# Selector products on 96 rows, and low products last behind a wait of their own

## The chip, the cores and the metric

The kernel runs on one core of one Trainium2 chip. The metric is the device time of one execution in microseconds (us). The core's engines are TensorE (PE: matrix products, with its weight loads listed apart as PEld), VectorE (DVE), ScalarE (ACT), GpSimd (POOL) and SyncE (SP, which here only issues DMAs). Each engine works off its own list of instructions in order. They meet only at semaphores: an instruction may wait until a counter has reached a value.

## The reference

Two blocks run one after the other on 64 images of 1024 channels and 14 x 14 points, all in float32. The first is three convolutions with batch norm over the whole batch. The second, in which the change lies, works on each image by itself:

```python
def _L1_conv_ref(x, w1, gn1_scale, gn1_bias, w_off, b_off, w2, gn2_scale, gn2_bias, w3, gn3_scale, gn3_bias, stride):
    out = relu(group_norm(conv(x, w1), gn1_scale, gn1_bias))      # 1024 -> 256 channels
    om = conv(out, w_off, pad=1) + b_off                          # 27 channels, 3x3
    off_x, off_y, mask = om[:, :9], om[:, 9:18], sigmoid(om[:, 18:])
    py, px = grid_y + off_y, grid_x + off_x                       # a point for each tap
    sampled = bilinear_sample(out, py, px) * mask                 # 9 taps
    out = einsum('bckhw,ock->bohw', sampled, w2)                  # deformable 3x3, 256 -> 256
    out = relu(group_norm(out, gn2_scale, gn2_bias))
    out = group_norm(conv(out, w3), gn3_scale, gn3_bias)          # 256 -> 1024 channels
    return relu(out + x)
```

## The kernel before

**Stages.** Three phases do the first block (to about 900 us of the span). `deformable_phase` does the second. It goes through 32 pairs of images; a pair has 2 x 196 = 392 columns.

**Split products.** Each float32 operand is stored as two parts in a matmul type: `hi`, a rounded copy that ScalarE makes, and `lo`, what is left, which VectorE makes as value minus `hi`. So `lo` is always later than `hi`. A product of two operands is three matmuls into one sum: w_hi x_hi, w_hi x_lo, w_lo x_hi. `product3` (lines 69 to 74) issues them in that order; in every view below L72, L73 and L74 are these three. A matmul loads its own stationary operand.

**The steps of a pair on TensorE:**
- `conv1(p, k)`, k = 0 to 7: 1x1 convolution from 1024 to 256 channels, two output tiles of `work`, 6 matmuls for each k. It waits for `x1_lo_made`.
- `offsets`: the 27 channel convolution, into `work`.
- `spread_offsets(p, c)`, c = 0 to 2 (line 1999): one matmul each with 0/1 matrices `select`, which hands each offset channel to the partitions of its taps and rows. Its input `om_parts` has 64 rows: 32 with the high part of the offsets, 32 with the low part. ScalarE then makes from the results the weights of the bilinear sampling ("hats"), and these go through DRAM back into SBUF. There are 3 x 32 = 96 of these matmuls.
- `transposes(p, i)`: four float32 matmuls each, into `work`.
- `sample_tile(p, t)`, t = 0 to 19: bilinear sampling as a product of the activations `aT` with the sampling matrix `s` over 98 rows, 6 matmuls, into one of two banks of `sample`. `s` comes in 9 units a pair: GpSimd multiplies two hats, ScalarE makes `s_hi`, VectorE `s_lo` (L1793). The first tile of each unit (channel half c == 0, 10 tiles a pair) waits for `s_lo_made`. Every tile also waits with `at_least(pe, v_lo_made, ...)` for the bank of `sample` to be read.
- `deform_part(p, g, part)`: the deformable product over two taps (one in the last group), into `deform`. ScalarE makes `v_hi` from `sample` (L1447), VectorE `v_lo` (L1801). Ten of the twenty parts a pair wait for `v_lo_made`.
- `conv3(p, k)`, k = 0 to 7: 256 to 1024 channels, 6 matmuls each. The first of each k waits for `y_written` (its bank of `work` read), the first of all for `b_lo_made` too.
- `group_a`, `group_b`, `group_y`: small matmuls for the group norms (L1123), into `sums_ps`.

**Order.** The order on each engine is written out by hand in its `step` function. One step interleaves parts of four neighbouring pairs, so that while VectorE and ScalarE prepare one thing TensorE has another. `keep_warm` adds matmuls whose results are not used, at the beginning and the end.

In the built program each matmul carries the size of the part of TensorE's array that it uses, as rows x columns. It is 128x128 for all matmuls of the kernel (those with 98 rows in `sample_tile` and those with 96 columns in `offsets` among them), except the 96 of `spread_offsets`, which carry 64x128. 2,283 matmuls have a wait.

Of the kernel before, what the change touches and what calls it, by code (L numbers as in the profile page):

```python
# [14 lines left out]
F32R = mybir.dt.float32r  # L15
# [32 lines left out]
OFFCH = 27  # L48
ONE = 29
# [6 lines left out]
def at_least(eng, sem, value):  # L56

    if not isinstance(value, int) or value > 0:
        eng.wait_ge(sem, value)
# [17 lines left out]
def keep_warm(nc, out, values, count):  # L77

    for _ in range(count):
        nc.tensor.matmul(out, values[:, 0:P], values[:, 0:PAIR], start=True, stop=True)  # L80

# [1077 lines left out]
def deformable_phase(nc, x, y3, before_layer, w1, w2, w3_source, woff_source, consts, hats_at, out, y_home, in_home, y_stored, x1,  # L1159
# [4 lines left out]
    with ExitStack() as ctx:  # L1164
# [36 lines left out]

        a_hi = x1_hi[:].rearrange("p r i s -> p (r i s)")[:, 0:KM * PAIR].rearrange("p (k i s) -> p k i s", k=KM, i=2)
        a_lo = x1_lo[:].rearrange("p r i s -> p (r i s)")[:, 0:KM * PAIR].rearrange("p (k i s) -> p k i s", k=KM, i=2)
        om_parts = x1_hi[0:64, RING - 1].rearrange("p i s -> p (i s)")
# [53 lines left out]
        select, place = consts["select"][0:64, :], consts["select"][64:96, 0:PIX]  # L1258
# [703 lines left out]
        def _(pe):  # L1962
            @of_pair
            def conv1(p, k):
                if k == 0:
                    at_least(pe, aT_lo_made, 2 * p.n - 1)
                    at_least(pe, y_written, KX * (p.n - 2))
                pe.wait_ge(x1_lo_made, KX * p.n + k + 1)
                for t in range(KM):
                    last = product3(nc, work[:, t, 0:PAIR], w1_hi[:, k, t, :], w1_lo[:, k, t, :],  # L1970
                                    x1_hi[:, k % RING].rearrange("p i s -> p (i s)"),
                                    x1_lo[:, k % RING].rearrange("p i s -> p (i s)"),
                                    start=(k == 0), stop=(k == KX - 1))
                last.then_inc(conv1_used, 1)
# [39 lines left out]
            @of_pair  # L2014
            def sample_tile(p, t):
                g, i, c = t // 4, t // 2 % 2, t % 2
                u, n = min(t // 2, UNITS - 1), cols(g)
                at = i * PIX if u == UNITS - 1 else 0
                unit = UNITS * p.n + u
                if t in (0, 2):  # L2020
                    pe.wait_ge(aT_lo_made, 2 * p.n + i + 1)
                if c == 0:
                    pe.wait_ge(s_lo_made, unit + 1)
                at_least(pe, v_lo_made, TILES * p.n + t - 1)
                for h in range(2):
                    last = product3(nc, sample[:, t % 2, 0:n], aT_hi[:, i, h, c * P:(c + 1) * P],
                                    aT_lo[:, i, h, c * P:(c + 1) * P],
                                    s_hi[:, unit % 2, h, at:at + n], s_lo[:, unit % 2, h, at:at + n],
                                    start=(h == 0), stop=(h == 1))
                last.then_inc(sampled, 1)  # L2030

            @of_pair
            def deform_part(p, g, part):
                k, t = divmod(part, 2)
                group = GROUPS * p.n + g
                if t == 0:
                    pe.wait_ge(v_lo_made, TILES * p.n + 4 * g + 3 + k)
                if part == 0 and g == 0:
                    at_least(pe, b_raw, p.n)
                for tap in range(taps_of(g)):  # L2040
                    last = product3(nc, deform[:, t, 0:PAIR], w2_hi[:, k, 2 * g + tap, t, :],
                                    w2_lo[:, k, 2 * g + tap, t, :],
                                    v_hi[:, group % 2, k, tap].rearrange("p i s -> p (i s)"),
                                    v_lo[:, group % 2, k, tap].rearrange("p i s -> p (i s)"),
                                    start=(g == 0 and k == 0 and tap == 0),
                                    stop=(g == GROUPS - 1 and k == KM - 1 and tap == taps_of(g) - 1))
                if t == 1:
                    last.then_inc(deformed, 1)

            @of_pair  # L2050
            def conv3(p, k):
                bank = 2 - k % 2
                if k == 0:
                    if p.n == 0:
                        pe.wait_ge(w3.lo_made, 1)
                    pe.wait_ge(b_lo_made, p.n + 1)
                    pe.wait_ge(aT_lo_made, 2 * min(p.n + 2, PAIRS))
                if k == 1:
                    pe.wait_ge(a_raw, min(p.n + 3, PAIRS))
                at_least(pe, y_written, KX * p.n + k - 1)  # L2060
                for c in range(KM):
                    last = product3(nc, work[:, bank, 0:PAIR], w3_hi[:, c, k, :], w3_lo[:, c, k, :],
                                    b_hi[:, c, :], b_lo[:, c, :], start=(c == 0), stop=(c == KM - 1))
                last.then_inc(conv3_done, 1)
# [110 lines left out]
def build(nc, x, w, vectors, select, ident, ones, b_off, out):  # L2175
# [5 lines left out]
    with ExitStack() as ctx:  # L2181
# [3 lines left out]
        select_s = sb("select_s", [96, 3 * TAPS * SIDE], F32R)  # L2185
# [21 lines left out]
        with ExitStack() as inner:  # L2207
# [22 lines left out]
            stage = in_home[0:96, 0:3 * TAPS * SIDE]  # L2230
# [66 lines left out]
```

## Time and profile before

| what | value |
|---|---|
| three runs | 2995.97, 2997.18, 2997.70 us, median 2997.18 us |
| the profiled execution's own time | 2997.73 us |
| its span, first to last instruction | 2995.6 us |
| PE busy | 2936.5 us (98%), 16,518 matmuls |
| DVE busy | 2374.3 us (79%) |
| ACT busy | 1798.1 us (60%) |
| POOL busy | 717.0 us (24%) |
| mean granted clock of TensorE | 0.993 of full |

The profiled execution lies 0.5 us above the median and 2.1 us above its own span. A matmul of 392 columns is listed with 0.34 us, but the next one starts 0.18 us after it: matmuls overlap, so the distance from start to start, not the busy time, is what one costs. Idle time is counted from the end of one matmul to the start of the next, so a wait listed with 0.57 us moved the next start by more than that.

### The profile page before, as it was taken

The page shows a single profiled execution, that of the slowest core. Times are in us where ns is not written, and L with a number is a line of the kernel's source. Part 1 is how long each engine was busy: PE and PEld are TensorE (multiplying, and loading weights), DVE is VectorE, ACT ScalarE, POOL GpSimd, SP SyncE. Part 2 cuts the span into 40 slices and gives each one's busy share as a digit, 9 for nine tenths or more (in the row PEclk, how much of TensorE's full clock was granted, in tenths as well). Part 3 has the DMA queues.
Part 4 walks back from the last instruction along what each step waited for, and adds up shares of the span by engine and source line. Part 5 has one row for each costly group of instructions (what it writes and reads, how often), then busy time and mean ns, then how long its engine had stood idle before and what let it go on. Part 6 is the DMA issues. An engine that isn't in the chain of part 4 may idle for free.

```text
span 2995.6 us, 46528 instructions
## 1 busy us (share of the span) xinstructions
PE 2936.5 (98%) x16518; PEld 2861.0 (96%) x16518; DVE 2374.3 (79%) x4872; ACT 1798.1 (60%) x3281; POOL 717.0 (24%) x433
## 2 busy tenths in 40 slices
PE   9999999999998999999999999999999999999997
PEld 9999999999997999999999999999999999999997
DVE  5755888965665688888888888888888888888875
ACT  4544332246654566676666766667666676666664
POOL 0000000000001333333333333333333333333331
PEclk9999999999999999999999999999999999999998
DMA  7774111035653354444444444444444444444431
GB/s 270 217 232 128 44 44 44 22 127 221 256 214 115 119 163 145 145 153 147 157 146 148 155 149 148 151 150 146 155 150 152 152 141 148 148 160 148 143 113 73
DMA packets 209175, 437.34 MB, mean 146 GB/s; under 512 B 18640, under 2 KB 170160, under 8 KB 203312
## 3 DMA queue, kind: packets, MB, share of 16 engines
q1 hardware_dynamic: 159376, 326.77, 32.4%
q10 hardware_dynamic: 49568, 107.60, 11.2%
q8 instruction: 131, 2.15, 0.3%
q14 instruction: 100, 0.82, 0.1%
HBM read 307.66 MB, written 126.64 MB: 145 GB/s over the span
## 4 chain that ended last, share of the span: by engine, by line
PE 58%; DVE 9%; ACT 1%; issue 0%; DMA 0%; POOL 0%; ACTq 0%; DVEq 0%; POOLq 0%
PE work L72 7%; PE work L74 7%; PE sample L72 6%; PE work L73 6%; PE deform L72 6%; PE sample L74 6%; PE sample L73 6%; PE deform L73 6%; PE deform L74 6%; DVE s_lo L1793 2%; DVE x L1817 2%; DVE x_lo L1705 1%; DVE v_lo L1801 1%; DVE x L1699 1%; PE work L2010 1%; PE work L1999 1%
## 5 line engine op out<-in xcount | busy, mean ns | idle before, releaser
L1655 POOL TENSOR_TENSOR hats<-hats 98x784 f32<-98x784 f32 x288 | 602.6, 2092 | 887.2 <-DMA hats<-hat_scratch 857.4
L1447 ACT ACTIVATE v_hi<-sample 128x392 fp32r<-128x392 f32 (+1 forms) x640 | 295.5, 462 | 337.5 <-PE sample L74 318.8
L72 PE MATMUL sample<-s_hi,aT_hi 98*128 98x392 f32 (+1 forms) x1280 | 426.6, 333 | 18.4 <-DVE s_lo L1793 13.5
L73 PE MATMUL sample<-s_lo,aT_hi 98*128 98x392 f32 (+1 forms) x1280 | 419.6, 328 | 0.0
L74 PE MATMUL sample<-s_hi,aT_lo 98*128 98x392 f32 (+1 forms) x1280 | 419.3, 328 | 0.0
L72 PE MATMUL deform<-v_hi,w_w 128*128 128x392 f32 x1152 | 406.4, 353 | 0.9 <-DVE v_lo L1801 0.7
L73 PE MATMUL deform<-v_lo,w_w 128*128 128x392 f32 x1152 | 392.7, 341 | 0.0
L74 PE MATMUL deform<-v_hi,w_w 128*128 128x392 f32 x1152 | 391.6, 340 | 0.0
L1801 DVE TENSOR_TENSOR v_lo<-sample,v_hi 128x392 fp32r<-128x392 f32 (+1 forms) x640 | 327.1, 518 | 74.6 <-ACT v_hi L1447 73.0
L1793 DVE TENSOR_TENSOR s_lo<-hats,s_hi 98x784 fp32r<-98x784 f32 x288 | 346.6, 1204 | 2.6 <-ACT s_hi L1438 1.6
L1438 ACT ACTIVATE s_hi<-hats 98x784 fp32r<-98x784 f32 x288 | 245.6, 853 | 104.3 <-DVE x L1699 77.4
L72 PEld LDWEIGHTS sample<-s_hi,aT_hi 98*128 98x128 f32 x1280 | 241.4, 189 | 34.7 <-DVE s_lo L1793 21.1
L73 PEld LDWEIGHTS sample<-s_lo,aT_hi 98*128 98x128 f32 x1280 | 242.6, 190 | 0.0
L74 PEld LDWEIGHTS sample<-s_hi,aT_lo 98*128 98x128 f32 x1280 | 241.9, 189 | 0.0
L72 PEld LDWEIGHTS deform<-v_hi,w_w 128*128 128x128 f32 x1152 | 217.0, 188 | 8.3 <-issue 5.8
L1817 DVE SCALAR_TENSOR_TENSOR x<-y_home,gn,x 128x196 f32<-128x196 f32 x496 | 220.5, 505 | 0.1
L288 POOL TENSOR_TENSOR bn<-bn,half_neg 128x2 f32<-128x2 f32 (+1 forms) x3 | 3.0, 1012 | 904.8 <-DVE bn L307 622.1
L73 PEld LDWEIGHTS deform<-v_lo,w_w 128*128 128x128 f32 x1152 | 217.4, 189 | 0.0
L74 PEld LDWEIGHTS deform<-v_hi,w_w 128*128 128x128 f32 x1152 | 216.6, 188 | 0.0
L1705 DVE TENSOR_TENSOR x_lo<-x,x_hi 128x392 fp32r<-128x392 f32 x256 | 199.9, 781 | 9.8 <-ACT x_hi L1379 9.8
L1699 DVE SCALAR_TENSOR_TENSOR x<-in_home,scale,x 128x392 f32<-128x392 f32 x248 | 196.2, 792 | 6.2 <-DMA in_home<-y_scratch 6.1
L1503 ACT ACTIVATE x<-x,gn 128x196 f32<-128x196 f32 x496 | 191.6, 448 | 0.7 <-DVE x L1817 0.4
(226 smaller groups left out, 7349.0 us busy)
## 6 DMA issues: line engine op xcount, KB each, us to landing
hats<-hat_scratch SPq DMA_DIRECT2D x768, 150.1 KB
x<-in_x SPq DMA_DIRECT2D x64, 784.0 KB, 5.9
in_home<-y_scratch ACTq DMA_DIRECT2D x248, 196.0 KB, 2.9
out<-x ACTq DMA_DIRECT2D x62, 784.0 KB, 3.4
y_home<-in_x SPq DMA_DIRECT2D x32, 784.0 KB, 5.0
y_scratch<-y_out SPq DMA_DIRECT2D x16, 1568.0 KB, 5.9
terms<-in_x SPq DMA_DIRECT2D x30, 784.0 KB, 4.7
y_scratch<-y_home SPq DMA_DIRECT2D x15, 1568.0 KB, 5.2
```

Source lines behind the costliest of these rows:

```text
L72: nc.tensor.matmul(out, w_hi, x_hi, start=start, stop=False)
L73: nc.tensor.matmul(out, w_hi, x_lo, start=False, stop=False)
L74: return nc.tensor.matmul(out, w_lo, x_hi, start=False, stop=stop)
L1438: nc.scalar.activation(s_hi[:, unit % 2], hats[:, unit % HATS, 0:2], ACT.Copy).then_inc(s_hi_made, 1)
L1447: nc.scalar.activation(v_hi[:, group % 2, c, 0:taps_of(g), i, :], sample[:, t % 2, 0:cols(g)].rearrange("p (k s) -> p k s", s=PIX), ACT.Co ...
L1503: last = nc.scalar.activation(x1[:, p.buf, i, k, :], x1[:, p.buf, i, k, :], ACT.Relu, bias=gn3.shift[:, i, k:k + 1])
L1655: nc.gpsimd.tensor_tensor(hats[:, slot, 0:2, 0:n], hats[:, slot, 0:2, 0:n], hats[:, slot, 2:3, 0:n].broadcast_to([HALF, 2, n]), ALU.mult). ...
L1699: nc.vector.scalar_tensor_tensor(x1[:, p.buf, :, k, :], from_y, scale[:, k:k + 1], x1[:, p.buf, :, k, :], ALU.mult, ALU.add).then_inc(plus ...
L1705: nc.vector.tensor_tensor(x1_lo[:, k % RING], x1[:, p.buf, :, k, :], x1_hi[:, k % RING].bitcast(F32), ALU.subtract).then_inc(x1_lo_made, 1)
L1793: nc.vector.tensor_tensor(s_lo[:, unit % 2], hats[:, unit % HATS, 0:2], s_hi[:, unit % 2].bitcast(F32), ALU.subtract).then_inc(s_lo_made, 1)
L1801: nc.vector.tensor_tensor(v_lo[:, group % 2, c, 0:taps_of(g), i, :], sample[:, t % 2, 0:cols(g)].rearrange("p (k s) -> p k s", s=PIX), v_h ...
L1817: last = nc.vector.scalar_tensor_tensor(x1[:, p.buf, i, k, :], y[:, i, k, :], gn3.scale[:, i, k:k + 1], x1[:, p.buf, i, k, :], ALU.mult, A ...
```

## The change

**Rows.** `om_parts` and `select` have 96 rows in place of 64. The 32 new rows of `select` hold zeros; the 32 new rows of `om_parts` are what stands in that part of `x1_hi`. The table `place`, which stood in rows 64 to 95 of the same tensor, moves to rows 96 to 127, so the tensor is loaded and copied with 128 rows in place of 96. The matmuls of `spread_offsets` now carry 128x128 as all others do.

**Order of products.** In `conv1`, `sample_tile`, `deform_part` and `conv3`, `product3` is replaced by `products_of_high` (w_hi x_hi and w_lo x_hi) for all tiles, taps or halves of the call, and after them `product_of_low` (w_hi x_lo) for all. The wait at the head is now for the high part; a wait for the low part stands before the first low product. `offsets` keeps `product3`. The number of matmuls is the same. The matmuls with a wait are 3,211 in place of 2,283: 928 more, 320 in `sample_tile`, 320 in `deform_part`, 256 in `conv1` and 32 in `conv3`. The lists of the other engines have the same number of entries as before.

```diff
+SPREAD_ROWS = 96
+def products_of_high(nc, out, w_hi, w_lo, x_hi, start):
+    nc.tensor.matmul(out, w_hi, x_hi, start=start, stop=False)
+    nc.tensor.matmul(out, w_lo, x_hi, start=False, stop=False)
+
+def product_of_low(nc, out, w_hi, x_lo, stop):
+    return nc.tensor.matmul(out, w_hi, x_lo, start=False, stop=stop)
...
-        om_parts = x1_hi[0:64, RING - 1].rearrange("p i s -> p (i s)")
+        om_parts = x1_hi[0:SPREAD_ROWS, RING - 1].rearrange("p i s -> p (i s)")
...
-        select, place = consts["select"][0:64, :], consts["select"][64:96, 0:PIX]
+        select, place = consts["select"][0:SPREAD_ROWS, :], consts["select"][SPREAD_ROWS:P, 0:PIX]
...
+                pe.wait_ge(x1_hi_made, KX * p.n + k + 1)
+                for t in range(KM):
+                    products_of_high(nc, work[:, t, 0:PAIR], w1_hi[:, k, t, :], w1_lo[:, k, t, :],
+                                     x1_hi[:, k % RING].rearrange("p i s -> p (i s)"), start=(k == 0))
                 pe.wait_ge(x1_lo_made, KX * p.n + k + 1)
                 for t in range(KM):
-                    last = product3(nc, work[:, t, 0:PAIR], w1_hi[:, k, t, :], w1_lo[:, k, t, :],
-                                    x1_hi[:, k % RING].rearrange("p i s -> p (i s)"),
-                                    x1_lo[:, k % RING].rearrange("p i s -> p (i s)"),
-                                    start=(k == 0), stop=(k == KX - 1))
+                    last = product_of_low(nc, work[:, t, 0:PAIR], w1_hi[:, k, t, :],
+                                          x1_lo[:, k % RING].rearrange("p i s -> p (i s)"), stop=(k == KX - 1))
                 last.then_inc(conv1_used, 1)
...
                 if c == 0:
-                    pe.wait_ge(s_lo_made, unit + 1)
+                    pe.wait_ge(s_hi_made, unit + 1)
                 at_least(pe, v_lo_made, TILES * p.n + t - 1)
                 for h in range(2):
-                    last = product3(nc, sample[:, t % 2, 0:n], aT_hi[:, i, h, c * P:(c + 1) * P],
-                                    aT_lo[:, i, h, c * P:(c + 1) * P],
-                                    s_hi[:, unit % 2, h, at:at + n], s_lo[:, unit % 2, h, at:at + n],
-                                    start=(h == 0), stop=(h == 1))
+                    products_of_high(nc, sample[:, t % 2, 0:n], aT_hi[:, i, h, c * P:(c + 1) * P],
+                                     aT_lo[:, i, h, c * P:(c + 1) * P], s_hi[:, unit % 2, h, at:at + n], start=(h == 0))
+                if c == 0:
+                    pe.wait_ge(s_lo_made, unit + 1)
+                for h in range(2):
+                    last = product_of_low(nc, sample[:, t % 2, 0:n], aT_hi[:, i, h, c * P:(c + 1) * P],
+                                          s_lo[:, unit % 2, h, at:at + n], stop=(h == 1))
...
                 if t == 0:
-                    pe.wait_ge(v_lo_made, TILES * p.n + 4 * g + 3 + k)
+                    pe.wait_ge(v_hi_made, TILES * p.n + 4 * g + 3 + k)
...
                 if k == 0:
...
-                    pe.wait_ge(b_lo_made, p.n + 1)
+                    pe.wait_ge(b_hi_made, p.n + 1)
...
+                if k == 0:
+                    pe.wait_ge(b_lo_made, p.n + 1)
...
-        select_s = sb("select_s", [96, 3 * TAPS * SIDE], F32R)
+        select_s = sb("select_s", [P, 3 * TAPS * SIDE], F32R)
```

Place 1, TensorE, in the middle of a pair's step: the first part of `deform_part` of group 0 and, behind it, `sample_tile` 4, the first tile of unit 2 of `s`. Before:

```order
L72 MATMUL deform<-v_hi,w_w 128x392 [waits b_raw,v_lo_made]
L73 MATMUL deform<-v_lo,w_w 128x392
L74 MATMUL deform<-v_hi,w_w 128x392
L72 MATMUL deform<-v_hi,w_w 128x392
L73 MATMUL deform<-v_lo,w_w 128x392
L74 MATMUL deform<-v_hi,w_w 128x392
L72 MATMUL sample<-s_hi,aT_hi 128x392 [waits v_lo_made,s_lo_made]
L73 MATMUL sample<-s_lo,aT_hi 128x392
L74 MATMUL sample<-s_hi,aT_lo 128x392
L72 MATMUL sample<-s_hi,aT_hi 128x392
L73 MATMUL sample<-s_lo,aT_hi 128x392
L74 MATMUL sample<-s_hi,aT_lo 128x392
```

After (L86 and L87 are the two high products, L91 the low one):

```order
L86 MATMUL deform<-v_hi,w_w 128x392 [waits b_raw,v_hi_made]
L87 MATMUL deform<-v_hi,w_w 128x392
L86 MATMUL deform<-v_hi,w_w 128x392
L87 MATMUL deform<-v_hi,w_w 128x392
L91 MATMUL deform<-v_lo,w_w 128x392 [waits v_lo_made]
L91 MATMUL deform<-v_lo,w_w 128x392
L86 MATMUL sample<-s_hi,aT_hi 128x392 [waits v_lo_made,s_hi_made]
L87 MATMUL sample<-s_hi,aT_lo 128x392
L86 MATMUL sample<-s_hi,aT_hi 128x392
L87 MATMUL sample<-s_hi,aT_lo 128x392
L91 MATMUL sample<-s_lo,aT_hi 128x392 [waits s_lo_made]
L91 MATMUL sample<-s_lo,aT_hi 128x392
```

The wait for `s_lo_made` moved from the first matmul of the tile to the fifth; four matmuls now stand between the wait for `s_hi_made` and it. The same holds for `v_lo_made` in the deformable product ahead.

Place 2, TensorE, one `conv1` step in the same iteration. Before:

```order
L72 MATMUL work<-x_hi,w_w 128x392 [waits x1_lo_made]
L73 MATMUL work<-x_lo,w_w 128x392
L74 MATMUL work<-x_hi,w_w 128x392
L72 MATMUL work<-x_hi,w_w 128x392
L73 MATMUL work<-x_lo,w_w 128x392
L74 MATMUL work<-x_hi,w_w 128x392
```

After:

```order
L86 MATMUL work<-x_hi,w_w 128x392 [waits x1_hi_made]
L87 MATMUL work<-x_hi,w_w 128x392
L86 MATMUL work<-x_hi,w_w 128x392
L87 MATMUL work<-x_hi,w_w 128x392
L91 MATMUL work<-x_lo,w_w 128x392 [waits x1_lo_made]
L91 MATMUL work<-x_lo,w_w 128x392
```

The two tiles of `work` take their four high products first, and the wait for `x1_lo_made` stands before the last two matmuls.

## Rows read from the trace of the kernel before

**Rows 1.** the page: its first line and its section 1 (busy us, share, instructions).
```profile
span 2995.6 us, 46528 instructions
...
PE 2936.5 (98%) x16518; PEld 2861.0 (96%) x16518; DVE 2374.3 (79%) x4872; ACT 1798.1 (60%) x3281; POOL 717.0 (24%) x433
```

**Rows 2.** busy us in a stretch: PE, PEld, DVE, ACT, POOL, PEclk, DMA share, GB/s.
```profile
1400.00:2400.00 1000.00, 993.65 (x5721) 970.45 (x5719) 859.73 (x1959) 687.18 (x1400) 356.66 (x208) 1.00 0.47 150
```

**Rows 3.** waits of TensorE, whole span: us in total, times, longest us.
```profile
PE sample L72 <- DVE s_lo L1793: 13.5, 17, 1.2
PE work L72 <- DVE x_lo L1705: 9.1, 4, 3.1
...
PE sample L72 <- DVE v_lo L1801: 4.7, 7, 1.7
PE work L72 <- DVE b_lo L1756: 2.2, 1, 2.2
...
PE deform L72 <- DVE v_lo L1801: 0.7, 2, 0.4
```

**Rows 4.** timeline of TensorE around one spread: start us, us.
```profile
2000.72 0.34 PE L74 MATMUL sample<-s_hi,aT_lo 98*128 98x392 f32 x1
2000.89 0.34 PE L72 MATMUL work<-b_hi,w3b_w 128*128 128x392 f32 x1
...
2001.79 0.34 PE L74 MATMUL work<-b_hi,w3b_w 128*128 128x392 f32 x1
2002.06 0.44 PE L1999 MATMUL work<-x_hi,select_s 64*126 64x392 f32 x1
2002.34 0.33 PE L1999 MATMUL sums_ps<-x_hi,select_s 64*126 64x392 f32 x1
2002.60 0.44 PE L72 MATMUL sample<-s_hi,aT_hi 98*128 98x392 f32 x1
2002.88 0.34 PE L73 MATMUL sample<-s_lo,aT_hi 98*128 98x392 f32 x1
...
2003.60 0.34 PE L74 MATMUL sample<-s_hi,aT_lo 98*128 98x392 f32 x1
2003.87 0.44 PE L1999 MATMUL work<-x_hi,select_s 64*126 64x392 f32 x1
2004.23 0.44 PE L72 MATMUL deform<-v_hi,w_w 128*128 128x392 f32 x1
2004.51 0.34 PE L73 MATMUL deform<-v_lo,w_w 128*128 128x392 f32 x1
```

**Rows 5.** timeline of the weight loads in the same stretch: start us, us.
```profile
2001.61 0.19 PEld L74 LDWEIGHTS work<-b_hi,w3b_w 128*128 128x128 f32 x1
2002.06 0.18 PEld L1999 LDWEIGHTS work<-x_hi,select_s 64*126 64x126 f32 x1 [0.26 <-issue]
```

**Rows 6.** timeline of TensorE at one late low part of `s`.
```profile
1845.02 0.34 PE L74 MATMUL deform<-v_hi,w_w 128*128 128x392 f32 x1
1845.93 0.45 PE L72 MATMUL sample<-s_hi,aT_hi 98*128 98x392 f32 x1 [0.57 <-DVE s_lo L1793]
1846.22 0.34 PE L73 MATMUL sample<-s_lo,aT_hi 98*128 98x392 f32 x1
```

**Rows 7.** timeline of VectorE at two such low parts.
```profile
1843.51 2.36 DVE L1793 TENSOR_TENSOR s_lo<-hats,s_hi 98x784 fp32r<-98x784 f32 x1
...
2033.37 0.96 DVE L1793 TENSOR_TENSOR s_lo<-hats,s_hi 98x784 fp32r<-98x784 f32 x1
```

**Rows 8.** timeline of GpSimd at the first of them.
```profile
1843.14 1.91 POOL L1655 TENSOR_TENSOR hats<-hats 98x784 f32<-98x784 f32 x1 [2.80 <-DMA hats<-hat_scratch]
```

**Rows 9.** waits of VectorE from 1400 to 2400 us.
```profile
DVE gn L1135 <- PE sums_ps L1123: 27.2, 32, 1.4
```

**Rows 10.** costliest groups: busy us, mean ns of one | idle before.
```profile
L72 PE MATMUL deform<-v_hi,w_w 128*128 128x392 f32 x1152 | 406.4, 353 | 0.9 <-DVE v_lo L1801 0.7
L73 PE MATMUL deform<-v_lo,w_w 128*128 128x392 f32 x1152 | 392.7, 341 | 0.0
```

More of the change, by code:

```diff
@@ L2040, in deform_part @@
                 for tap in range(taps_of(g)):
[L2041 to L2046, printed above, removed]
+                    products_of_high(nc, deform[:, t, 0:PAIR], w2_hi[:, k, 2 * g + tap, t, :], w2_lo[:, k, 2 * g + tap, t, :],
+                                     v_hi[:, group % 2, k, tap].rearrange("p i s -> p (i s)"),
+                                     start=(g == 0 and k == 0 and tap == 0))
+                if t == 0:
+                    pe.wait_ge(v_lo_made, TILES * p.n + 4 * g + 3 + k)
+                for tap in range(taps_of(g)):
+                    last = product_of_low(nc, deform[:, t, 0:PAIR], w2_hi[:, k, 2 * g + tap, t, :],
+                                          v_lo[:, group % 2, k, tap].rearrange("p i s -> p (i s)"),
+                                          stop=(g == GROUPS - 1 and k == KM - 1 and tap == taps_of(g) - 1))
                 if t == 1:
@@ L2061, in conv3 @@
                 for c in range(KM):
-                    last = product3(nc, work[:, bank, 0:PAIR], w3_hi[:, c, k, :], w3_lo[:, c, k, :],
-                                    b_hi[:, c, :], b_lo[:, c, :], start=(c == 0), stop=(c == KM - 1))
+                    products_of_high(nc, work[:, bank, 0:PAIR], w3_hi[:, c, k, :], w3_lo[:, c, k, :], b_hi[:, c, :],
+                                     start=(c == 0))
+                if k == 0:
+                    pe.wait_ge(b_lo_made, p.n + 1)
+                for c in range(KM):
+                    last = product_of_low(nc, work[:, bank, 0:PAIR], w3_hi[:, c, k, :], b_lo[:, c, :], stop=(c == KM - 1))
                 last.then_inc(conv3_done, 1)
@@ L2229, in build @@
             points.place(x1[:, 2:4].rearrange("p b i k s -> p (b i k s)")[:, 0:3 * POINT], raw)
-            stage = in_home[0:96, 0:3 * TAPS * SIDE]
+            stage = in_home[:, 0:3 * TAPS * SIDE]
             conv1_phase(nc, x_v, w1, w["w1a"], points, w["w2a"], constants, (select_s, select, stage), half_neg, homes,
@@ L2263 @@
     woff[..., 0:OFFCH] = a["L1_conv_w_off"].reshape(OFFCH, P, KM, 3, 3).transpose(1, 2, 3, 4, 0)
-    select = np.zeros((96, 3, TAPS, SIDE), np.float32)
+    select = np.zeros((P, 3, TAPS, SIDE), np.float32)
     for tap in range(TAPS):
@@ L2269 @@
         select[ONE, 1, tap] = tap % 3 - 1 - np.arange(SIDE)
-    select = select.reshape(96, 3 * TAPS * SIDE)
-    select[64:64 + TAPS, 0:PIX] = np.tile(np.arange(SIDE), SIDE)
-    select[64 + TAPS:64 + 2 * TAPS, 0:PIX] = np.repeat(np.arange(SIDE), SIDE)
+    select = select.reshape(P, 3 * TAPS * SIDE)
+    select[SPREAD_ROWS:SPREAD_ROWS + TAPS, 0:PIX] = np.tile(np.arange(SIDE), SIDE)
+    select[SPREAD_ROWS + TAPS:SPREAD_ROWS + 2 * TAPS, 0:PIX] = np.repeat(np.arange(SIDE), SIDE)
     b_off = np.zeros((32, 1), np.float32)
```

## The prediction

> **What bounds the kernel now.** I read the page first. TensorE is busy 98% of the span [rows 1], so almost any time that leaves the total must leave TensorE's list. A stretch of the second block shows the same: 993.65 of 1000 us on TensorE at the full granted clock, VectorE at 860 us, ScalarE at 687 [rows 2]. The change removes no matmul, so at first sight nothing can be won. But busy time hides gaps here, because matmuls overlap: each is listed with 0.34 us and the next starts 0.18 us later. From 2000.72 to 2001.79 six starts pass in 1.07 us, 0.178 us each [rows 4]. So the second view is the timeline, read from start to start: where does a start come later than 0.178 us after the one before? There are two kinds of places.
>
> The first is around the matmuls with 64 rows. Starts there are 0.26 to 0.36 us apart with no wait named [rows 4]. The second is behind real waits; the list of waits gives 13.5 us for `s_lo` in 17 places, 9.1 us for the low part of x1 in 4, 4.7 us for the bank of `sample`, 2.2 us for `b_lo`, 0.7 us for `v_lo` in the deformable product [rows 3]. Both kinds are what the change touches.
>
> **Part 1: 96 rows in place of 64.** From the last matmul before the first two spread matmuls (2001.79) to the second matmul behind them (2002.88) four starts take 1.09 us; at 0.178 us they would take 0.71. From 2003.60 over the third spread to 2004.51 three starts take 0.91 us in place of 0.53. Each place costs 0.38 us over the pitch, 0.76 us a pair [rows 4]. The weight loads say why: in the ordinary stream a load begins one matmul ahead (the load for the matmul at 2001.79 begins at 2001.61), but that of the first spread begins at 2002.06 with its own matmul, after 0.26 us without any load [rows 5]. Going from a matmul that uses 128x128 of the array to one that uses 64x128, and back, stops the overlap. The wait on the spread is not the reason: coming back to `sample` at 2002.60 is as slow as going in, and the step out to the deformable product at 2004.23 is the slowest (0.36 us).
>
> After the change the three spreads carry 128x128 like their neighbours, and four switches a pair are gone. The spreads stay, at 0.178 us each. Saved: 0.76 x 32 = 24.3 us. No row shows a matmul with 96 rows; the nearest are those of `sample` with 98, which follow 128-row ones at the ordinary pitch (2000.72 to 2000.89) [rows 4]. The bounds are 0 (96 rows stop the stream as 64 do) and 24.3; I take 24.3, since 98 rows is the nearest row and the two carry the same array size. The Trainium skill, TensorEngine Tiling (Array Packing), Key Properties, says that a change of tiling mode drains the engine, and its list of configurations has 32, 64 and 128 rows and none of 96; no run here shows the list.
>
> A rule speaks against this. The Trainium skill, TensorE: Matmul & The Clock Gate, The mechanism (Part 3), has a weight load run beside a matmul only when the two use different row groups. By it every product here would expose its load, and 96 rows, which overlap their neighbours' groups as 64 rows do, would win nothing. The trace disagrees: loads of 128 rows start beside matmuls of 128 rows throughout.
>
> The longer copy and load of `select` happen once, in the first block, with the same columns per partition. I cost them at nothing: TensorE's list does not touch them before the spread of the first pair. At most they add a fraction of a microsecond at the start.
>
> **Part 2: low products last.** What a wait costs is more than its idle time. At 1845.02 to 1845.93 the listed idle is 0.57 us, but the start moved by 0.91 - 0.18 = 0.73, and the next start is 0.29 us on, another 0.11 [rows 6]. So a wait of x costs x + 0.16 + 0.11. The 17 waits for `s_lo` cost 13.5 + 17 x 0.27 = 18.1 us.
>
> Why it is late: VectorE needs 0.96 us for `s_lo` when alone and 2.36 at 1843.51, where GpSimd's multiply had begun at 1843.14 and ended at 1845.05 [rows 7, 8]. In such pairs `s_lo` is ready just after TensorE wants it. `s_hi` must be ready before `s_lo` begins, so at least 0.96 us and here 2.36 us earlier. After the change TensorE starts the four high products at once and reaches the low ones 4 x 0.178 = 0.71 us later. A mean wait moved the start by 13.5/17 + 0.16 = 0.95 us; 0.24 of it is left, plus 0.11 for starting again: 0.35 x 17 = 6.0 us. Saved 12.1 us.
>
> The other three by the same cover: `v_lo` in the deformable product, two waits of 0.35 us on average, go wholly (0.7 + 2 x 0.27 = 1.2 us). The four x1 waits and the one for `b_lo` are longer than the cover (up to 3.1 us), and each gives back 0.71: 2.8 and 0.7 us. These fall where the pipeline fills and empties, where VectorE's own pace decides, so the tail behind the last low part (2 matmuls in place of 6) is what counts. Sum of part 2: 12.1 + 1.2 + 2.8 + 0.7 = 16.8 us. The bounds are 0 (each saved wait turns up elsewhere) and all of it: 13.5 + 9.1 + 2.2 + 0.7 + 24 x 0.27 = 32.0 us.
>
> What is late next: the wait for the bank of `sample` (4.7 us, 7 times [rows 3]) is not moved. It needs the low part of the tile two before, and a TensorE that waits less elsewhere comes to it earlier. I give back 2 us for it, somewhat under half of its present cost. VectorE's list does not become the bound: it has 140 us of idle time in 1000 [rows 2], and waits for TensorE's group sums twice a pair, 27.2 us over 32 times [rows 9], so its timing is tied to TensorE's again in each pair and does not fall behind for good.
>
> **What the added waits cost.** 928 matmuls get a wait that they did not have. Behind each low product that waits stand one or more low products, then all of the list. A wait that is already met costs nothing where I can see it: the first matmul of `conv3` at 2000.89 waits for `y_written` and starts 0.17 us after the one before [rows 4]. An upper bound comes from the deformable products: L72, which carries the waits, takes 12 ns more on average than L73, 1152 x 12 = 13.8 us [rows 10]; the switches back from the third spread explain 32 x 0.10 = 3.2 of them, and the rest over 320 waits is 0.033 us each, or 31 us for 928. Below is 0. I take 0, the value of the row that shows one met wait.
>
> **Sum.** 2997.7 - 24.3 - 16.8 + 2 = 2958.6 us against the profiled execution. The median of the runs is 0.5 us below that execution, so I forecast 2958 us, 1.3% under the median. The case's own range is 2948 to 2972: down by most of the waits vanishing, up by the waits giving nothing (2974) or met waits costing 0.01 to 0.015 us each.
>
> **Rivals.**
> - *The waits come back.* TensorE's saved time turns into waits at other low parts, since VectorE and ScalarE keep their pace. For it: VectorE is at 86% [rows 2], and `s_lo` is late by chance of overlap with GpSimd, whose phase moves. Against it: VectorE waits for TensorE in each pair. Part 1 stays: 2997.2 - 24.3 = 2973 us.
> - *96 rows are not 128.* The switches stay, part 2 is as forecast: 2997.2 - 14.8 = 2982 us. For it: no row shows 96 rows. Against: the neighbours with 98.
> - *Slower: a wait in the middle of a group breaks the stream even when met.* A real wait leaves the next load exposed, 0.11 us [rows 6]. If each of the 928 did that, 102 us come on top of the forecast: 3060 us. It decides from 0.042 us a wait on (39 us / 928). The bound from the deformable products is 0.033, and the row of `conv3` shows none, so this is unlikely.
>
> **How the numbers follow.** Forecast 0.80, waits come back 0.10, no gain from the rows 0.05, slower by waits 0.03, the rest 0.02. Leaving out the last two and the far end of the third, the range is 2946 to 2976. About 0.2% (6 us) is what a measurement of this kernel can tell from no change. Faster by more than that: the first three cases, 0.95. Slower by more: 0.03. Within: 0.02.
>
> **What the profile after would show.** The timeline around a spread has 0.18 us from start to start, and the first load no longer follows a gap; no matmul is listed with 64 rows. Ends of pairs are some 0.76 us closer. The waits of TensorE name `s_lo` at the low product, fewer than 10 times and under 0.7 us each, with a total of 5 us or less; `x_lo` stays near 6 us. Waits for the bank of `sample` grow a little from 4.7 us. Wrong would be: starts of 0.26 us around the spreads; starts over 0.2 us at low products whose wait is met; or a total of TensorE's waits as large as now.

## The result and the profile after

The changed kernel takes 2978.6 us (median of 5 runs, 2972.6 to 2981.2) against 2997.2 us before (5 runs, 2992.7 to 3001.2): the ratio is 0.9938, with a 95% interval of 0.9928 to 0.9949. The forecast was 2958 us and the range ended at 2976: the direction is right, the gain is about half of what was forecast (18.6 of 39 us).

The page of the changed kernel, the row of the engines:

```profile
PE 2915.8 (98%) x16518; PEld 2864.6 (96%) x16518; DVE 2397.4 (81%) x4872; ACT 1795.9 (60%) x3281; POOL 712.0 (24%) x433
```

One stretch of the second block (columns as in [rows 2]):

```profile
1400.00:2400.00 1000.00, 991.33 (x5752) 979.91 (x5751) 878.77 (x1969) 690.50 (x1409) 355.96 (x209) 1.00 0.47 151
```

VectorE is busy 879 us of these 1000; before it was 860 [rows 2].

**The spreads.** The timeline of TensorE around a spread (start us, us):

```profile
1995.71 0.33 PE L2013 MATMUL sums_ps<-x_hi,select_s 96*126 96x392 f32 x1
1995.89 0.34 PE L86 MATMUL sample<-s_hi,aT_hi 98*128 98x392 f32 x1
...
1996.60 0.52 PE L91 MATMUL sample<-s_lo,aT_hi 98*128 98x392 f32 x2
1996.96 0.34 PE L2013 MATMUL work<-x_hi,select_s 96*126 96x392 f32 x1
1997.13 0.35 PE L86 MATMUL deform<-v_hi,w_w 128*128 128x392 f32 x1
1997.32 0.34 PE L87 MATMUL deform<-v_hi,w_w 128*128 128x392 f32 x1
```

and its weight loads in front of it:

```profile
1995.36 0.19 PEld L2013 LDWEIGHTS work<-x_hi,select_s 96*126 96x126 f32 x1
1995.54 0.19 PEld L2013 LDWEIGHTS sums_ps<-x_hi,select_s 96*126 96x126 f32 x1
```

All starts are now 0.17 to 0.19 us apart, and each load begins one matmul ahead, where before there were 0.26 to 0.36 us and a load that began with its own matmul [rows 4, 5]. So a pair without any wait is shorter. The same matmul (the second spread) of two consecutive pairs, first in the kernel before:

```profile
2189.95 0.33 PE L1999 MATMUL sums_ps<-x_hi,select_s 64*126 64x392 f32 x1
...
2252.15 0.33 PE L1999 MATMUL sums_ps<-x_hi,select_s 64*126 64x392 f32 x1
```

and in the changed kernel:

```profile
2182.17 0.34 PE L2013 MATMUL sums_ps<-x_hi,select_s 96*126 96x392 f32 x1
...
2243.63 0.33 PE L2013 MATMUL sums_ps<-x_hi,select_s 96*126 96x392 f32 x1
```

62.20 us have become 61.46, 0.74 less; 0.76 was worked out.

**The waits.** In mid-stage (1000 to 2900 us of the span) the waits of TensorE were, before (us in total, times, longest us):

```profile
PE sample L72 <- DVE s_lo L1793: 12.5, 15, 1.2
PE sample L72 <- DVE v_lo L1801: 1.3, 2, 0.9
PE deform L72 <- DVE v_lo L1801: 0.3, 1, 0.3
```

and are after:

```profile
PE sample L91 <- DVE s_lo L1805: 7.1, 12, 1.2
PE sums_ps L1134 <- DVE gn L1129: 4.9, 7, 0.8
PE sample L86 <- DVE v_lo L1813: 1.0, 1, 1.0
```

They total 14.1 us before and 13.0 after, not far from what the prediction itself had named as a sign of being wrong, a total as large as before. Those for `s_lo` stand at the low product now (L91), but there are still 12, 7.1 us in total and up to 1.2 us long, where fewer than 10, under 0.7 us each and 5 us in total were forecast; and TensorE waits 7 times for the group sums, which it never did in mid-stage before. The mean pair (the last 29 distances between second spreads) went from 62.93 to 62.33 us, 0.60 less, though a pair without waits lost 0.74.

One wait for `s_lo`, in a pair whose second spread starts at 1620.67. TensorE:

```profile
1620.67 0.33 PE L2013 MATMUL sums_ps<-x_hi,select_s 96*126 96x392 f32 x1
...
1652.76 0.34 PE L86 MATMUL sample<-s_hi,aT_hi 98*128 98x392 f32 x1
...
1653.30 0.33 PE L87 MATMUL sample<-s_hi,aT_lo 98*128 98x392 f32 x1
1654.53 0.63 PE L91 MATMUL sample<-s_lo,aT_hi 98*128 98x392 f32 x2 [0.90 <-DVE s_lo L1805]
```

VectorE ahead of it:

```profile
1644.48 0.68 DVE L1797 TENSOR_TENSOR aT_lo<-work,aT_hi 98x512 fp32r<-98x512 f32 x1
...
1647.39 3.05 DVE L1829 SCALAR_TENSOR_TENSOR x<-y_home,gn,x 128x196 f32<-128x196 f32 x4
1650.36 0.61 DVE L1711 SCALAR_TENSOR_TENSOR x<-in_home,scale,x 128x392 f32<-128x392 f32 x1
...
1651.85 2.62 DVE L1805 TENSOR_TENSOR s_lo<-hats,s_hi 98x784 fp32r<-98x784 f32 x1
```

GpSimd at the same time:

```profile
1647.26 1.95 POOL L1667 TENSOR_TENSOR hats<-hats 98x784 f32<-98x784 f32 x1 [4.27 <-DMA hats<-hat_scratch]
1651.75 1.89 POOL L1667 TENSOR_TENSOR hats<-hats 98x784 f32<-98x784 f32 x1 [2.54 <-DMA hats<-hat_scratch]
```

In the pair before the change whose second spread began at 1812.63, TensorE would have begun sample tile 4 at 1845.20 (one pitch behind [rows 6]), 32.57 us after it, and needed `s_lo` at once. Now the tile begins 32.09 us after the spread (1652.76), and the first low product is due at 1653.48, 32.81 us after it. The four high products were to give `s_lo` 0.71 us more; measured from the spread they give 0.24 in these two pairs. The rest went into TensorE's coming sooner. VectorE did not come sooner: over 24 pairs its `s_lo` of unit 2 ends 32.74 us after the second spread before the change, and 32.88 us after it now. From 1644.48 to 1654.40 the timeline of VectorE shows no idle time (over the 24 pairs there are 0.03 us of it in this stretch before, 0.09 now), and GpSimd holds it twice, at 1647.26 (four `x<-y_home` take 3.05 us; most take 0.41 each) and 1651.75 (`s_lo` takes 2.62 us in place of 0.96).

The other new wait, for the group sums. TensorE:

```profile
2060.52 0.51 PE L91 MATMUL deform<-v_lo,w_w 128*128 128x392 f32 x2
2061.81 0.36 PE L1134 MATMUL sums_ps<-gn,ones_s 128*128 128x4 f32 x2 [0.78 <-DVE gn L1129]
```

VectorE:

```profile
2057.21 2.44 DVE L1805 TENSOR_TENSOR s_lo<-hats,s_hi 98x784 fp32r<-98x784 f32 x1
2059.57 0.62 DVE L1742 BATCH_NORM_STATS2 gn<-y_home 128x6 f32<-128x196 f32 x2
2060.22 0.99 DVE L1121 TENSOR_TENSOR gn<-gn 128x32 f32<-128x32 f32 x1
...
2061.48 0.19 DVE L1129 TENSOR_REDUCE gn<-gn 128x2 f32<-128x32 f32 x1
```

GpSimd:

```profile
2056.94 1.87 POOL L1667 TENSOR_TENSOR hats<-hats 98x784 f32<-98x784 f32 x1 [4.54 <-DMA hats<-hat_scratch]
2060.13 1.03 POOL L1674 TENSOR_TENSOR offs_b<-offs_b 126x392 f32<-126x392 f32 x1 [1.31 <-ACT offs_b L1435]
```

`s_lo` of unit 7 stands ahead of the last statistics of gn3 on VectorE, and GpSimd's multiply stretches it to 2.44 us. The first step of the reduction (L1121, median 0.20 us) then meets GpSimd's next operation, the masks at 2060.13, and takes 0.99 us. The statistics end at 2061.67, while TensorE is due at 2060.88, one pitch behind the second of the two low products. Undisturbed, TensorE asks for these sums 4.13 us after the second spread before the change and 3.56 us after it now; the latest statistics end at 4.12 before, just in time, and at 4.35 now.

### The profile page after: what moved, and what is told of

Its sections match the earlier page's. It is cut to its first block, busy times and chain, and to the rows that moved or that the text cites. A ratio compares the mean times of both kernels' runs of the same rounds, so it can differ in the third digit from the quotient of the medians.

```text
span 2976.6 us, 46528 instructions
## 1 busy us (share of the span) xinstructions
PE 2915.8 (98%) x16518; PEld 2864.6 (96%) x16518; DVE 2397.4 (81%) x4872; ACT 1795.9 (60%) x3281; POOL 712.0 (24%) x433
## 4 chain that ended last, share of the span: by engine, by line
PE 56%; DVE 10%; ACT 1%; issue 0%; DMA 0%; POOL 0%; ACTq 0%; SPq 0%; DVEq 0%; POOLq 0%
PE sample L86 6%; PE sample L91 6%; PE deform L86 6%; PE deform L91 6%; PE sample L87 6%; PE deform L87 6%; PE work L86 5%; PE work L91 5%; PE work L87 5%; DVE s_lo L1805 3%; DVE x L1829 2%; DVE x L1711 1%; DVE x_lo L1717 1%; DVE v_lo L1813 1%; PE work L73 1%; PE work L75 1%
## 5 line engine op out<-in xcount | busy, mean ns | idle before, releaser
L86 PE MATMUL sample<-s_hi,aT_hi 98*128 98x392 f32 (+1 forms) x1280 | 418.1, 332 | 6.4 <-DVE v_lo L1813 6.1
L87 PE MATMUL sample<-s_hi,aT_lo 98*128 98x392 f32 (+1 forms) x1280 | 412.7, 328 | 0.0
L86 PE MATMUL deform<-v_hi,w_w 128*128 128x392 f32 x1152 | 403.7, 350 | 0.0
L87 PE MATMUL deform<-v_hi,w_w 128*128 128x392 f32 x1152 | 393.2, 341 | 0.0
L1805 DVE TENSOR_TENSOR s_lo<-hats,s_hi 98x784 fp32r<-98x784 f32 x288 | 360.1, 1251 | 2.7 <-ACT s_hi L1450 1.7
L91 PE MATMUL sample<-s_lo,aT_hi 98*128 98x392 f32 (+1 forms) x1280 | 316.4, 328 | 7.1 <-DVE s_lo L1805 7.1
L91 PE MATMUL deform<-v_lo,w_w 128*128 128x392 f32 x1152 | 310.7, 342 | 0.0
L86 PEld LDWEIGHTS sample<-s_hi,aT_hi 98*128 98x128 f32 x1280 | 241.1, 188 | 13.6 <-issue 7.9
L87 PEld LDWEIGHTS sample<-s_hi,aT_lo 98*128 98x128 f32 x1280 | 242.5, 189 | 0.1
L91 PEld LDWEIGHTS sample<-s_lo,aT_hi 98*128 98x128 f32 x1280 | 226.0, 189 | 12.1 <-DVE s_lo L1805 12.1
L1829 DVE SCALAR_TENSOR_TENSOR x<-y_home,gn,x 128x196 f32<-128x196 f32 x496 | 227.3, 520 | 0.1
L87 PEld LDWEIGHTS deform<-v_hi,w_w 128*128 128x128 f32 x1152 | 218.0, 189 | 0.0
L86 PEld LDWEIGHTS deform<-v_hi,w_w 128*128 128x128 f32 x1152 | 217.7, 189 | 0.0
L1711 DVE SCALAR_TENSOR_TENSOR x<-in_home,scale,x 128x392 f32<-128x392 f32 x248 | 207.9, 839 | 9.6 <-DMA in_home<-y_scratch 9.5
L91 PEld LDWEIGHTS deform<-v_lo,w_w 128*128 128x128 f32 x1152 | 211.9, 188 | 0.4 <-DVE v_lo L1813 0.3
L1717 DVE TENSOR_TENSOR x_lo<-x,x_hi 128x392 fp32r<-128x392 f32 x256 | 187.6, 734 | 7.9 <-ACT x_hi L1391 7.1
```

Source lines behind the costliest of these rows:

```text
L86: nc.tensor.matmul(out, w_hi, x_hi, start=start, stop=False)
L87: nc.tensor.matmul(out, w_lo, x_hi, start=False, stop=False)
L91: return nc.tensor.matmul(out, w_hi, x_lo, start=False, stop=stop)
L1711: nc.vector.scalar_tensor_tensor(x1[:, p.buf, :, k, :], from_y, scale[:, k:k + 1], x1[:, p.buf, :, k, :], ALU.mult, ALU.add).then_inc(plus ...
L1717: nc.vector.tensor_tensor(x1_lo[:, k % RING], x1[:, p.buf, :, k, :], x1_hi[:, k % RING].bitcast(F32), ALU.subtract).then_inc(x1_lo_made, 1)
L1805: nc.vector.tensor_tensor(s_lo[:, unit % 2], hats[:, unit % HATS, 0:2], s_hi[:, unit % 2].bitcast(F32), ALU.subtract).then_inc(s_lo_made, 1)
```

## The experiments

Two theories are held against each other. A: the time saved on TensorE is met by VectorE, which GpSimd's operations hold up and whose list keeps its own pace from the transposes on. B: the waits added before the low products cost time in themselves.

Each was timed in rounds with the kernel before on the same chip. Waits quoted are those of TensorE between 1000 and 2900 us (us in total, times, longest us).

**1. The rows alone.** The kernel before with `om_parts` and `select` on 96 rows:

```diff
-        om_parts = x1_hi[0:64, RING - 1].rearrange("p i s -> p (i s)")
+        om_parts = x1_hi[0:SPREAD_ROWS, RING - 1].rearrange("p i s -> p (i s)")
```

> The kernel before with the 96-row selectors alone, product order and waits as before. Theory A (the saved time of the spreads is met by VectorE, whose list from the transposes on keeps its own pace): starts around the spreads fall to 0.18 us, but TensorE comes 0.57 us sooner to sample tile 4 and to the group sums, and the waits there grow; an undisturbed pair is near 61.5 to 62 us, the mean pair is only 0.2 to 0.4 us shorter than before, and the time is 2984 to 2992 us. Theory B (the low products' own waits cost time in themselves, so that the spreads' gain is whole without them): 24 us less than before, 2973 us or a little lower, with waits for s_lo as before (13 to 14 us).

Measured: 2989.9 us (11 runs), ratio 0.9974 [0.9964, 0.9984]: 7 us less, not 24.

```profile
PE sample L73 <- DVE s_lo L1794: 13.2, 15, 1.1
PE sums_ps L1124 <- DVE gn L1119: 5.7, 9, 0.8
PE deform L73 <- DVE v_lo L1802: 2.3, 7, 0.4
```

21.2 us of waits in place of 14.1, among them 9 for the group sums. The mean pair is 62.65 us, 0.27 less than before. Theory A's prediction holds, theory B's does not.

**2. The order of products alone.** The changed kernel with `SPREAD_ROWS = 64`:

```diff
-SPREAD_ROWS = 96
+SPREAD_ROWS = 64
```

> The changed order of products and the waits alone, spreads with 64 rows as before. Theory A: the cover of 0.71 us is whole here, because TensorE does not come sooner to sample tile 4; waits for s_lo fall from 13.5 us to under 5 us, and the time is 10 to 16 us under before, 2981 to 2987 us. Theory B (met waits in the middle of a group cost time): no gain or a loss, 2997 to 3003 us, and starts above 0.18 us at low products whose wait is met.

Measured: 2987.5 us (7 runs, 2982.0 to 2990.6), ratio 0.9970 [0.9958, 0.9981]: 9 us less, at the edge of what theory A expected. The profiled execution, the fastest of the seven (2982.0 us), has few waits left, 2.7 us in all:

```profile
PE sample L91 <- DVE s_lo L1805: 1.6, 2, 0.9
PE sample L86 <- DVE v_lo L1813: 0.9, 2, 0.6
```

GpSimd's hold falls on `s_lo` of unit 2 in only 6 of 24 pairs of this execution, against 11 before and 12 in the changed kernel, so a part of this small total is the luck of where GpSimd's multiply falls. The met waits are not the trouble: there is a gain, not a loss. And the two parts do not take from each other: alone they give 7 and 9 us, together 18.6. What is missing is missing from each alone: 17 of the 24.3 us of the rows, and 6 of the 14.8 us forecast for the order (16.8 less the 2 given back).

**3 to 5. VectorE without GpSimd's hold.** GpSimd multiplies only the first eighth of the columns of each hat, so that part of the computation is left out. Put into the kernel before, the one with the rows alone, and the changed one:

```diff
+                m = n // 8
-                nc.gpsimd.tensor_tensor(hats[:, slot, 0:2, 0:n], hats[:, slot, 0:2, 0:n],
-                                        hats[:, slot, 2:3, 0:n].broadcast_to([HALF, 2, n]), ALU.mult)
+                nc.gpsimd.tensor_tensor(hats[:, slot, 0:2, 0:m], hats[:, slot, 0:2, 0:m],
+                                        hats[:, slot, 2:3, 0:m].broadcast_to([HALF, 2, m]), ALU.mult)
```

> The kernel before, but GpSimd multiplies only the first eighth of the columns of each hat (the rest of the sampling matrix stays without its second factor). It tells whether VectorE is late at sample tile 4 because GpSimd's operations block it. If so (theory A), s_lo takes about 0.96 us everywhere, TensorE's waits for s_lo all but vanish, and the time is 13 to 20 us under before, 2977 to 2984 us. If VectorE is late by its own list, the waits for s_lo stay above 8 us and the time is within 6 us of before.

> The changed kernel with the same cut in GpSimd's multiplications (only the first eighth of the columns). Theory A: VectorE has room again, so the spreads' 24 us come through whole: 23 to 28 us under the kernel before with the same cut, near 2955 us, and pairs of 61.4 to 61.6 us throughout. If the changed kernel's shortfall has another cause (the added waits), the two cut kernels differ by no more than the two whole ones, 19 us, and waits of TensorE or slow starts at low products remain.

> The 96-row selectors alone with GpSimd's multiplications cut to an eighth of the columns, product order as before. If the rows are worth their 24 us whenever VectorE is in time, this is 22 to 25 us under the kernel before with the same cut (2973.1 us), 2948 to 2951 us, and the order of products has only the 2 to 5 us up to the changed kernel with the cut (2946.2 us) to itself. If the order has a gain of its own of the size forecast (about 17 us), it is near 2963 us.

Measured, with this cut: before 2973.1 us (0.9919 [0.9905, 0.9933] of the whole kernel before), rows alone 2948.8 (0.9841 [0.9825, 0.9857]), changed kernel 2946.2 (0.9834 [0.9819, 0.9848]). The first is 23 us under the whole kernel, more than the 13 to 20 expected. The only mid-stage wait for `s_lo` in the first cut kernel:

```profile
PE sample L72 <- DVE s_lo L1794: 0.7, 1, 0.7
```

Its `s_lo` from 1400 to 2400 us (duration min/median/max in ns):

```profile
L1794 DVE TENSOR_TENSOR s_lo<-hats,s_hi x144: 956/968/1176, 1407.9 to 2394.5; 98x784 fp32r<-98x784 f32 x144
```

And the changed kernel with the cut, the same stretch as [rows 2]:

```profile
1400.00:2400.00 1000.00, 1000.00 (x5834) 995.40 (x5833) 780.11 (x2004) 699.63 (x1429) 140.44 (x210) 1.00 0.48 153
```

In the kernel before with the cut `s_lo` never takes over 1.18 us in this stretch and TensorE's waits for it go from 12.5 us to 0.7; VectorE falls to 780 us in 1000 in the changed one. The cut also hands VectorE the product sooner, but that is not what helps: in the whole kernels (before, rows alone, changed) it stands idle for only 0.03 to 0.11 us a pair between `aT_lo` and the `s_lo` of unit 2, so it was not waiting for it.

With VectorE in time the rows are worth 2973.1 - 2948.8 = 24.3 us. Part 1 had 24.3; that the tenths agree is chance, as the two were timed in different rounds, and their ratios to the kernel before give 23.4. The traces show how it comes: between `aT_lo` and `s_lo` of unit 2 VectorE now has 1.1 us of idle time a pair, and when the rows bring TensorE 0.53 us sooner to sample tile 4 (from 32.59 to 32.06 us after the second spread), the end of `s_lo` follows by 0.53 us (31.58 to 31.05).

The order of products is then worth 2.5 us more, within what these rounds can tell apart. The traces place 0.9 us ahead of the third pair's second spread and 2.6 us behind the last one: filling and emptying, where 3.5 us had been worked out. Between them the mean pair is 61.50 us with the rows alone and 61.51 with the added waits too.

**6. The new order in the sampling tiles only.** 96 rows; `conv1`, `deform_part` and `conv3` go back to `product3` and its wait, as here:

```diff
-                    pe.wait_ge(v_hi_made, TILES * p.n + 4 * g + 3 + k)
+                    pe.wait_ge(v_lo_made, TILES * p.n + 4 * g + 3 + k)
...
-                    products_of_high(nc, deform[:, t, 0:PAIR], w2_hi[:, k, 2 * g + tap, t, :], w2_lo[:, k, 2 * g + tap, t, :],
+                    last = product3(nc, deform[:, t, 0:PAIR], w2_hi[:, k, 2 * g + tap, t, :],
```

> 96-row selectors and the new order of products in the sampling tiles alone; conv1, the deformable product and conv3 keep the old order. If nearly all of the order's gain lies in the waits for s_lo, this is within 4 us of the changed kernel (2975 to 2983 us). If the deformable product's and conv1's waits matter once the rows are changed (2.7 us of idle in 8 waits in the run with the rows alone, and 0.71 us at each x1 wait), it is 5 to 9 us slower than the changed kernel.

Measured: 2980.7 us (5 runs, 0.9951 [0.9937, 0.9965]), 2 us over the changed kernel and inside each other's spread. Against the rows alone (2989.9 us) the larger part of the order's gain comes from the sampling tiles; what `conv1`, the deformable product and `conv3` add is too small for this measurement.

**7. One step moved on VectorE, in the kernel before.**

```diff
                 add_x1(past, 7)
+                rest_s(now, 2)
+                rest_v(now, 2)
                 add_y(after, 5)
                 rest_x1(after, 4)
-                rest_v(now, 2)
-                rest_s(now, 2)
                 rest_v(now, 3)
```

> The kernel before with one step moved on VectorE: s_lo of unit 2 and v_lo of tile 2 are made before add_y(5) and x_lo(4), not after them. Nothing else changes. If VectorE's lateness at sample tile 4 is what TensorE pays for, s_lo is ready some 1.5 us sooner and mostly before GpSimd's multiply begins, the 15 waits for it go, and the time is 12 to 18 us under before, 2979 to 2985 us. If a blocked operation only moves to another place in the list, the time stays within 6 us of before.

Measured: 2992.0 us (12 runs), 0.9984 [0.9972, 0.9996]: 4 to 5 us, where 12 to 18 were expected. The waits for `s_lo` went, 12.5 us of them, but others came:

```profile
PE sample L72 <- DVE v_lo L1801: 5.2, 12, 0.8
```

Seven of these twelve are at the tile behind, sample tile 5, which needs `v_lo` of tile 3 before its first product. One such place, VectorE, GpSimd and TensorE:

```profile
2092.09 0.96 DVE L1793 TENSOR_TENSOR s_lo<-hats,s_hi 98x784 fp32r<-98x784 f32 x1
...
2093.45 2.24 DVE L1699 SCALAR_TENSOR_TENSOR x<-in_home,scale,x 128x392 f32<-128x392 f32 x1
...
2096.09 0.55 DVE L1801 TENSOR_TENSOR v_lo<-sample,v_hi 128x392 fp32r<-128x392 f32 x1
```

```profile
2093.38 1.89 POOL L1655 TENSOR_TENSOR hats<-hats 98x784 f32<-98x784 f32 x1 [2.10 <-DMA hats<-hat_scratch]
```

```profile
2096.70 0.45 PE L72 MATMUL sample<-s_hi,aT_hi 98*128 98x392 f32 x1 [0.70 <-DVE v_lo L1801]
```

`s_lo` of unit 2 runs ahead of GpSimd's multiply now and takes 0.96 us in every pair. The hold falls on what stands behind it, here `add_y` (2.24 us in place of 0.61), and that delays the next `v_lo`.

**8. The same step moved in the changed kernel.**

> The changed kernel with the same step moved on VectorE. Theory A (the shortfall is VectorE's place at sample tile 4 and at the group sums): the s_lo waits (12 places, 7.1 us of idle) go, the ones for the group sums stay, pairs of 61.5 us with seven of 62.5, and the time is 8 to 12 us under the changed kernel, 2966 to 2971 us. If another of VectorE's results is late at once, it stays within 4 us of the changed kernel.

Measured: 2975.0 us (5 runs), 0.9925 [0.9910, 0.9940], 4 us under the changed kernel and within its spread: a miss against the 8 to 12 us expected, by the same exchange. Of its 12 waits for `v_lo`, 11 are at sample tile 5.

```profile
PE sums_ps L1134 <- DVE gn L1129: 7.4, 12, 0.8
PE sample L86 <- DVE v_lo L1813: 6.3, 12, 1.2
```

**9. `s_lo` of unit 7 after the statistics, with and without step 7.** In the changed kernel:

```diff
                 count_y(before, 6)
-                rest_s(now, 7)
                 count_y(before, 7)
                 reduce_y(before)
                 rest_v(now, 11)
+                rest_s(now, 7)
                 moments(before, gn3, 8)
```

> The changed kernel with s_lo of unit 7 after the last statistics of gn3 on VectorE, the rest as it is. The mid-stage waits for the group sums (7 places, 6.0 us of delay) should go, those at sample tile 4 stay: 5 to 8 us under the changed kernel, 2970 to 2974 us. If TensorE's time before tile 4 comes back as longer waits there, within 3 us of the changed kernel.

> The changed kernel with that step moved and with s_lo of unit 7 made after the last statistics of gn3 in place of before them, so that GpSimd's hold on VectorE there no longer stands ahead of the group sums. Theory A: the waits of TensorE for the group sums in mid-stage (7 places, 6 us) shrink too, most pairs are at 61.5 us, and the time is 2958 to 2966 us. If ScalarE's copy of the last conv3 result sets the statistics, not VectorE's list, nothing is won over the kernel with the first step moved alone.

Measured: alone 2967.6 us (4 runs), 0.9900 [0.9883, 0.9918], 11 us under the changed kernel, more than the 5 to 8 expected; with step 7 as well 2968.4 us (5 runs), 0.9909 [0.9893, 0.9925], no better, where 2958 to 2966 was expected. In the kernel with this step alone no mid-stage wait for the group sums is left, and 12 for `s_lo` stay:

```profile
PE sample L91 <- DVE s_lo L1805: 5.2, 12, 1.1
```

With step 7 as well, those 12 turn into 14 longer ones for `v_lo`, 12 of them at sample tile 5:

```profile
PE sample L86 <- DVE v_lo L1813: 11.6, 14, 1.7
```

**10. The order in which TensorE wants them.** Unit 7 late, and at sample tile 4 `v_lo` first (wanted at the first product), then `s_lo` (wanted at the fifth), then the x1 low part:

```diff
                 add_y(after, 5)
-                rest_x1(after, 4)
                 rest_v(now, 2)
                 rest_s(now, 2)
+                rest_x1(after, 4)
                 rest_v(now, 3)
```

> The changed kernel with s_lo of unit 7 late, and at sample tile 4 v_lo of tile 2 first, then s_lo of unit 2, then x_lo(4) (before: x_lo(4), v_lo, s_lo). TensorE wants v_lo of tile 2 at the first product of the tile and s_lo of unit 2 at the fifth, so this is the order in which they are wanted. Against the kernel with both moves but s_lo first (2968.4 us), the 12 waits for v_lo at that tile (10.7 us of delay) should mostly go: 2958 to 2964 us. If GpSimd's hold still falls on s_lo there, a part comes back as waits at the low product: 2964 to 2968 us.

Measured: 2956.5 us (4 runs, 2954.5 to 2958.0), 0.9868 [0.9849, 0.9887]. This beats both kernels, by 40 and 22 us. Its wait in mid-stage:

```profile
PE sample L86 <- DVE v_lo L1813: 1.7, 3, 0.8
```

Beside it stand only two waits for `b`, 2.7 us, at the end of the stage, which this shorter kernel reaches before 2900 us. The mean pair is 61.63 us. The trace shows more than the order in which results are wanted. With the x1 low part behind it, `s_lo` of unit 2 starts sooner (30.5 us after the second spread in place of 31.2) and mostly ahead of GpSimd's multiply: it is held in 1 of 24 pairs, against 12 in the changed kernel. GpSimd is then the one that waits:

```profile
1702.71 0.96 DVE L1805 TENSOR_TENSOR s_lo<-hats,s_hi 98x784 fp32r<-98x784 f32 x1
```

```profile
1702.84 3.06 POOL L1667 TENSOR_TENSOR hats<-hats 98x784 f32<-98x784 f32 x1 [2.29 <-DMA hats<-hat_scratch]
```

No run separates the two effects.

## Why the prediction was wrong

- **What bounds the kernel, and where gaps hide:** right. Both kinds of places moved; new waits for the group sums came on top.
- **Part 1, the rows, 24.3 us:** what the switches cost on TensorE, and why, was right. The switches are gone, 96 rows behave as 98 do, an undisturbed pair lost 0.74 us, and with VectorE in time the rows give 24.3 us. That this reaches the total was wrong: alone in the whole kernel the rows gave 7 us. The sentence of the Trainium skill (TensorE: Matmul & The Clock Gate, The mechanism) that loads overlap only across different row groups does not hold for the stream here (the loads of 96 rows at 1995.36 and 1995.54 begin beside matmuls of 128 rows). The same section also names a background weight buffer as a case in which a load is pulled ahead, which the prediction left out; no row here shows where a load goes.
- **Part 2, low products last, 16.8 us:** over-sized. For `s_lo` it left 6.0 us of 18.1; by its own sum the 12 waits left cost 7.1 + 12 x 0.27 = 10.3. The cover was measured on the timeline of the kernel before, and part 1 brings TensorE some 0.5 us sooner to sample tile 4, so an undisturbed tile has 0.24 us of it left. But that is not an overlap of the two parts by itself: alone the order gave only 9 us, and on top of the rows it gives 11 (2989.9 to 2978.6).
- **The step that failed:** "so its timing is tied to TensorE's again in each pair and does not fall behind for good". With it part 1 was counted in full. VectorE's idle time was read as a sum over a stage, 140 us in 1000. It lies elsewhere in the pair. From the low part of `aT` to `s_lo` of unit 2 there is next to none (0.09 us a pair), and the measured end of that `s_lo` did not move with TensorE (32.74 and 32.88 us after the spread). Also `s_lo` of unit 7 and the statistics just behind the spreads are such a run, which the prediction did not look at: TensorE asks for the group sums 0.57 us sooner, VectorE is not ready, and 4.9 us of new waits arose there. The 2 us set aside for waits elsewhere were put at the bank of `sample`, where waits went from 4.7 to 6.1 us over the whole span and stayed small in mid-stage (1.3 and 1.0 us).
- **The rivals:** the mechanism of "the waits come back", VectorE keeping its pace while GpSimd's phase moves, is the one that the runs show; it had a chance of 0.10. Its price was not right: it kept part 1 whole and gave up part 2 (2973 us), while the runs show both cut down. By the number alone "96 rows are not 128" (2982 us) is nearer, by luck: its mechanism is refuted by the timeline around the spreads. "Slower by waits" is refuted: with GpSimd's work cut the mean pair is 61.51 us with all 928 added waits and 61.50 without them.
- **The rest:** the filling and emptying of the pipeline, 3.5 us forecast, fits the 2.5 us that the order gives between the cut kernels, and the 0.9 and 2.6 us of their traces.

The tie to GpSimd is shown by the cut, and by where the long operations fall once the steps are moved. How often GpSimd's multiply falls on `s_lo` of unit 2 differs from pair to pair (over 1.5 us in 11 of 24 pairs before, 12 of 24 after); what sets its phase was not tested. It starts when its hats have arrived by DMA.

## What to carry to other kernels

Time taken out of the bounding engine is only kept where the engine that feeds it has idle time between its last wait for the first one and the result that is wanted; look there, in the timeline of one period, not at its busy share. Price each saving against that lead, also when it stands alone: here neither part kept its size by itself. When the bounding engine moves forward, put the feeder's list in the order in which its results are wanted, and look which operation then meets the other engine's hold; two such swaps were worth 22 us here, more than the change itself.

## What was unexpected

- Matmuls with 96 rows run in the stream of 128-row ones without a gap: 0.17 to 0.19 us from start to start and the load one matmul ahead, against 0.26 to 0.36 us with 64 rows.
- VectorE's `s_lo`, with two SBUF inputs, waits for the end of GpSimd's multiply when it starts just after it: it takes 2.3 to 2.6 us in place of 0.96, and shortening GpSimd's work took 23 us off the kernel before, though GpSimd is busy 24% of the time and no wait of TensorE names it. The Trainium skill, SBUF — State Buffer, SBUF: two separate sides, describes the port pair that the two share as an exclusive lock, held for the whole instruction by whichever starts first. The trace agrees: `s_lo` at 1651.85, just behind GpSimd's start at 1651.75, ends 0.83 us after GpSimd's end at 1653.64; and where `s_lo` starts first, at 1702.71 in the kernel of step 10, GpSimd's multiply takes 3.06 us in place of 1.9.
- Runs of the kernel before spread over 0.6% in all rounds together (2990 to 3009 us), and each cut kernel over under 0.2%.
